# A two-block sequence model on one core: convolution read from the PSUM bank, MLP squares on VectorE, a third x buffer, and all engine queues in another order

## The chip, the cores and the metric

The kernel runs on one core of a Trainium2 chip. The metric is the device time of one execution in microseconds (us). Engines: PE is TensorE (PEld its weight loads), DVE is VectorE, ACT is ScalarE, POOL is GpSimd, SP is SyncE, whose queue issues all DMAs here.

## What is computed

There are 16 sequences ("items") of 256 tokens by 128 features, all in float32. Each goes through the same layers:

```
x1 = x + layernorm(block(layernorm(x)))
out = x1 + layernorm(ffn(layernorm(x1)))
block:
  xm = mix(x);  n = rms_norm(xm);  value, gate = split(n @ in_proj)
  value = silu(causal_conv4(value) + conv_b)
  y = scan(value, A, xm @ B_proj, xm @ C_proj) + D * value
  xm = xm + (y * silu(gate)) @ out_proj
  xm = xm + square(relu(rms_norm(xm) @ m_fc)) @ m_proj
  xa = attention(rms_norm(mix(xm)))          # 16 heads, 4 key/value heads, rope
  xa = xa + square(relu(rms_norm(xa) @ a_fc)) @ a_proj
ffn:  h = silu(x @ w1) * (x @ w2);  h = gelu(h @ h1);  h = gelu(h @ h2);  h @ w3
```

The convolution runs along the tokens with 4 taps per channel: the output at token t uses tokens t-3 to t.

## The kernel before

An item's work is cut into short steps with names (`tin`, `inv`, `bc`, `conv`, ...), each a function of the item `i` and a part `k`. `ORDERS` is a table written out by hand that lists, for each engine, the names in the order in which that engine issues them; `_instances` numbers them, and `run` calls them one after the other. Nothing else sets the order: an engine that waits in one step holds back all that stand behind it in its list. Several items are under way at a time, in different layers. Steps of different engines meet through one semaphore per name (`S[name]`, `at(name, i, k)`).

The eight PSUM banks are handed out by a second table, `BANKS`. `BANKS_OF` says how many banks a PE step claims and which step, on another engine, gives them back; `claim` makes PE wait for that step. All matmuls are recorded at one line (L1170) and all transposes at another (L1187).

The steps that matter here, with their lines before the change:

- `loadx` (SP, L355) brings an item's x into one of two buffers `X`; `st0`, `ag0` (L892, L900), `r1` (POOL, L427 and L430), `xh` (L905), `xm` (L927) make the layer norm; `ss1` (ACT, L600), `r2` (POOL, L437 and L440) and `nrm` (L932, written over `X`) the RMS norm. `tin` transposes both on PE, `xnhi` (ACT, L609) and `xnlo` (DVE, L937) split the result into a high and a low part. Only then can `inv`, `gat`, `bc` (the products with in_proj, B and C) run.
- `va` (ACT, L617) copies the bank of `inv` into `vpad`, whose first three columns are zero. `conv` (DVE, L949 and L951) is the four taps on `vpad`: for two channel halves of 128x256, one tensor_scalar and three scalar_tensor_tensor each. `val` (ACT, L627) is the silu, `vt` and `xp` transpose it.
- `bcx` (ACT, L644) takes B and C out of PSUM, `cb` multiplies them, `m` (DVE, L961 and L962) multiplies with the decay table `LM`, `v` is the product with the values.
- `up`, `relu` (ACT, L668), `sq` (POOL, L476), `down` are the first MLP, `upb`, `relub` (L766), `sqb` (POOL, L512), `downb` the second. `relu` writes `hid` in SBUF, and gives the bank back.
- `mx` (DVE, L1064) are row maxima of the scores, `ex` (ACT, L726) exponentials, `sel` (POOL, L496) the causal masks, `pv` the product with v.
- `glo`, `hlo` (POOL, L542 and L547) write the low parts `gL` for the products `h1` and `h2` (24 matmuls per part each).

Before the first item's bulk work there is preparation: the DVE makes a decay per head in a chain of small operations (`dec`, L828 to L847), ACT and DVE make `LM` from it (`pex` on ACT, L579; `plm` on DVE, L852; 16 operations each), ACT and DVE split the raw weights (`phi`, L584 and L588; `plo`, L862 and L865), DVE folds scales into weights (`fold`), POOL and ACT scale and split the weights of the second network (`fsc`, `flo` on POOL, L414 and L419; `fhi` on ACT, L593).

Of the kernel before, what the change touches and what calls it, by code (L numbers as in the profile page):

```python
# [1510 lines left out]
```

## Time and profile before

| | |
|---|---|
| median of 3 runs | 976.28 us (975.53 to 977.0) |
| the profiled execution | 976.42 us |
| its span in the trace | 974.7 us |
| mean granted TensorE clock | 0.988 of full speed |
| busy: PE / DVE / ACT / POOL | 91% / 69% / 59% / 47% of the span |
| DMA | 8 tenths busy in the first fortieth of the span, 1 tenth in the second, 0 after |

The page of the profile gives each engine's busy time and forty slices of the span. The stretches say the same for windows that one chooses. The waits say for whom an engine stood idle. The timeline lists instructions by start time, with the idle time before them and who ended it in square brackets; merged rows have a count (x16). A group's row gives busy time and mean duration in ns.

### The profile page before, as it was taken

The page shows a single profiled execution, that of the slowest core. Times are in us where ns is not written, and L with a number is a line of the kernel's source. Part 1 is how long each engine was busy: PE and PEld are TensorE (multiplying, and loading weights), DVE is VectorE, ACT ScalarE, POOL GpSimd, SP SyncE. Part 2 cuts the span into 40 slices and gives each one's busy share as a digit, 9 for nine tenths or more (in the row PEclk, how much of TensorE's full clock was granted, in tenths as well). Part 3 has the DMA queues.
Part 4 walks back from the last instruction along what each step waited for, and adds up shares of the span by engine and source line. Part 5 has one row for each costly group of instructions (what it writes and reads, how often), then busy time and mean ns, then how long its engine had stood idle before and what let it go on. Part 6 is the DMA issues. An engine that isn't in the chain of part 4 may idle for free.

```text
span 974.7 us, 24913 instructions
## 1 busy us (share of the span) xinstructions
PE 888.5 (91%) x9248; PEld 758.0 (78%) x9248; DVE 667.8 (69%) x1803; ACT 578.2 (59%) x1220; POOL 460.0 (47%) x708
## 2 busy tenths in 40 slices
PE   0689989999999999998999999999999999989785
PEld 0667768787979888987878898888877887878575
DVE  5978969866777767758576884875776686746320
ACT  3644365766747557746565768567475575575532
POOL 1574344625543637435345545355263644463432
PEclk9999999999999999999999999999999999999899
DMA  8100000000000000000000000000000000000000
GB/s 280 59 17 7 7 7 2 7 1 13 7 13 7 13 2 7 13 12 6 12 7 2 17 2 12 8 12 7 12 2 2 2 13 1 13 1 13 12 3 9
DMA packets 17926, 15.71 MB, mean 16 GB/s; under 512 B 2064, under 2 KB 15760, under 8 KB 17552
## 3 DMA queue, kind: packets, MB, share of 16 engines
q1 hardware_dynamic: 17808, 14.12, 4.6%
q8 instruction: 76, 1.25, 0.5%
q14 instruction: 42, 0.34, 0.1%
HBM read 12.02 MB, written 2.10 MB: 14 GB/s over the span
## 4 chain that ended last, share of the span: by engine, by line
PE 64%; DVE 22%; issue 7%; ACT 3%; POOL 2%; DMA 1%; SPq 0%; POOLq 0%; DVEq 0%; ACTq 0%
PE pool L1170 59%; PE pool L1187 5%; DVE mneg L1064 2%; DVE val L951 2%; DVE M L961 1%; DVE M L962 1%; ACT PT L726 1%; DVE W L1018 1%; DVE val L949 1%; DVE gAB L1144 1%; DVE W L1020 1%; POOL PT L496 1%; DMA X<-in_x 1%; DVE LM L852 1%; DVE val L968 1%
## 5 line engine op out<-in xcount | busy, mean ns | idle before, releaser
L1064 DVE TENSOR_REDUCE mneg<-pool 128x2 f32<-128x512 f32 (+1 forms) x192 | 119.0, 683 | 54.7 <-PE pool L1170 54.7
L1170 PE MATMUL pool<-gH,w_h_hi 128*128 128x256 f32 x512 | 149.1, 291 | 4.8 <-POOL gL L542 2.2
L1170 PE MATMUL pool<-gL,w_h_hi 128*128 128x256 f32 x512 | 143.8, 281 | 0.0
L1170 PE MATMUL pool<-gH,w_h_lo 128*128 128x256 f32 x512 | 143.8, 281 | 0.0
L961 DVE TENSOR_TENSOR M<-pool,LM 128x512 f32<-128x512 f32 x128 | 87.6, 685 | 55.2 <-PE pool L1170 54.8
L726 ACT ACTIVATE PT<-pool 128x512 f32<-128x512 f32 x192 | 99.2, 603 | 31.8 <-PE pool L1170 31.5
L1170 PE MATMUL pool<-BC 64*128 64x256 f32 (+1 forms) x1024 | 111.4, 345 | 3.3 <-ACT PT L726 1.7
L496 POOL TENSOR_SCALAR_AFFINE_SELECT PT<-PT 128x256 f32<-128x256 f32 (+1 forms) x192 | 89.2, 488 | 42.4 <-ACT PT L726 39.0
L1170 PEld LDWEIGHTS pool<-BC 64*128 64x128 f32 x1024 | 87.6, 187 | 26.1 <-issue 14.1
L644 ACT ACTIVATE BC<-pool 128x512 f32<-128x512 f32 x128 | 75.6, 603 | 54.2 <-PE pool L1170 50.9
L1170 PEld LDWEIGHTS pool<-gH,w_h_hi 128*128 128x128 f32 x512 | 96.9, 189 | 7.2 <-issue 3.2
L1170 PEld LDWEIGHTS pool<-gL,w_h_hi 128*128 128x128 f32 x512 | 97.0, 189 | 0.2
L1170 PEld LDWEIGHTS pool<-gH,w_h_lo 128*128 128x128 f32 x512 | 96.8, 189 | 0.0
L542 POOL TENSOR_TENSOR gL<-gAB,gH 128x512 fp32r<-128x512 f32 x32 | 41.3, 1301 | 65.2 <-ACT gH L787 64.9
L547 POOL TENSOR_TENSOR gL<-gAB,gH 128x512 fp32r<-128x512 f32 x32 | 41.0, 1286 | 50.1 <-ACT gH L801 50.0
L1170 PE MATMUL pool<-M,xpad 128*32 128x256 f32 (+1 forms) x1024 | 54.8, 332 | 3.6 <-DVE M L962 3.6
L1170 PE MATMUL pool<-PT,Va 128*32 128x128 f32 (+1 forms) x1024 | 53.2, 338 | 5.1 <-POOL PT L496 5.1
L806 ACT ACTIVATE gAB<-pool 128x512 f32<-128x512 f32 x32 | 19.1, 598 | 63.5 <-PE pool L1170 63.4
L951 DVE SCALAR_TENSOR_TENSOR val<-vpad,cols,val 128x256 f32<-128x256 f32 x96 | 54.9, 612 | 0.4
L962 DVE TENSOR_TENSOR M<-pool,LM 128x256 f32<-128x256 f32 x128 | 53.0, 414 | 0.0
L1170 PE MATMUL pool<-xnH,w_B_hi 128*128 128x256 f32 x128 | 44.0, 344 | 4.4 <-DVE M L962 3.9
L512 POOL TENSOR_TENSOR hid<-hid 128x512 f32<-128x512 f32 x32 | 33.5, 1051 | 29.7 <-ACT hid L766 29.7
(235 smaller groups left out, 2428.0 us busy)
## 6 DMA issues: line engine op xcount, KB each, us to landing
X<-in_x SPq DMA_DIRECT2D x16, 128.0 KB, 2.1
x<-in_x SPq DMA_DIRECT2D x16, 128.0 KB, 2.2
out<-ob SPq DMA_DIRECT2D x16, 128.0 KB, 2.1
hid<-in_w_h SPq DMA_DIRECT2D x1, 1024.0 KB, 8.9
gAB<-in_w_h SPq DMA_DIRECT2D x1, 1024.0 KB, 9.4
PT<-in_w_B SPq DMA_DIRECT2D x1, 512.0 KB, 4.9
PT<-in_w_C SPq DMA_DIRECT2D x1, 512.0 KB, 6.4
Qs<-in_s SPq DMA_DIRECT2D x1, 512.0 KB, 5.0
```

The costliest lines, as they stand in the source:

```text
L496: g.affine_select(w, w, pattern=[[0, w.shape[1]], [1, P]], compare_op=ALU.is_ge, fill=0.0, base=0, channel_multiplier=-1).then_inc(S["sel" ...
L512: g.tensor_tensor(h, h, h, ALU.mult).then_inc(S["sqb"], 1)
L542: g.tensor_tensor(gL[:, J], gA[:, J], gH[:, J].bitcast(F32), ALU.subtract).then_inc(S["glo"], 1)
L547: g.tensor_tensor(gL[:, J], gB[:, J], gH[:, J].bitcast(F32), ALU.subtract).then_inc(S["hlo"], 1)
L644: a.activation(BC[:, n % NBC, :], bank("bc", i, k), ACT.Copy).then_inc(S["bcx"], 1)
L726: a.activation(PT[:, n % NPT, :], bank("e", i, k // 4, k % 4), ACT.Exp).then_inc(S["ex"], 1)
L951: last = v.scalar_tensor_tensor(dst, vpad[:, b, k:k + L], w, dst, ALU.mult, ALU.add)
L961: v.tensor_tensor(M[:, n % NM, :, 0:L], pool8[:, b:b + 2, 0:L], LM[:, 2 * k:2 * k + 2, :], ALU.mult)
L962: v.tensor_tensor(M[:, n % NM, :, L:3 * P], pool8[:, b:b + 2, L:3 * P], LM[:, 2 * k:2 * k + 2, 0:P], ALU.mult).then_inc(S["m"], 1)
L1064: v.reduce_max(dst, o, axis=AX.X, negate=True).then_inc(S["mx"], 1)
L1170: return p.matmul(o, lhsT, rhs, start=start, stop=True, skip_group_check=True)
L1187: last = p.transpose(o[:, k * P:(k + 1) * P], src(k), ident[:])
```

## The change

1. `va` and `vpad` are gone. `conv` reads the bank of `inv` itself. Tap 0 is now the one without a shift and writes all 256 columns with the bias; taps 1 to 3 read columns 0 to 255-k and add to columns k onwards, so no padding is needed. The bank is given back by the last `conv` instead of `va`.
2. `sq` and `sqb` go from POOL to DVE: one scalar_tensor_tensor of 128x512 computes max(bank, 0) times `hid`. ACT's relu stays. The banks of `up` and `upb` are now given back by `sq` and `sqb`.
3. `X` has three buffers; x of items 0 to 2 is loaded at the start. `rows` is loaded third instead of fifth, w_in no longer waits for it, and `m01` (DVE) waits for the first group of transfers only.
4. `xr` (POOL) has one more wait, for its own earlier step.
5. All five lists of `ORDERS` and the bank table are other ones.

```diff
-    tin=(1, "xnlo"), inv=(1, "va"), ...
-    t2=(1, "t2c"), up=(1, "relu"), ... upb=(1, "relub"),
+    tin=(1, "xnlo"), inv=(1, "conv"), ...
+    t2=(1, "t2c"), up=(1, "sq"), ... upb=(1, "sqb"),
...
         def conv(i, k):
-            if k == 0:
-                dve.wait_ge(S["va"], at("va", i))
+            if k == 0:
+                dve.wait_ge(S["inv"], at("inv", i))
...
             for b in range(2):
-                w, dst = cols[:, C_CW + b * KC + k:C_CW + b * KC + k + 1], val[:, i % 2, b, :]
+                c = C_CW + b * KC + KC - 1 - k
+                src, dst = halves(bank("inv", i))[:, b, 0:L - k], val[:, i % 2, b, k:]
                 if k == 0:
-                    last = v.tensor_scalar(dst, vpad[:, b, 0:L], w, cols[:, C_CB + b:C_CB + b + 1], ALU.mult, ALU.add)
+                    last = v.tensor_scalar(dst, src, cols[:, c:c + 1], cols[:, C_CB + b:C_CB + b + 1], ALU.mult, ALU.add)
                 else:
-                    last = v.scalar_tensor_tensor(dst, vpad[:, b, k:k + L], w, dst, ALU.mult, ALU.add)
+                    last = v.scalar_tensor_tensor(dst, src, cols[:, c:c + 1], dst, ALU.mult, ALU.add)
...
-        def va(i, _):
-            act.wait_ge(S["inv"], at("inv", i))
...
-            a.activation(vpad[:, :, KC - 1:], halves(bank("inv", i)), ACT.Copy).then_inc(S["va"], 1)
...
-        def sq(i, k):
-            pool.wait_ge(S["relu"], at("relu", i, k))
-            h = hid[:, 0, 2 * k:2 * k + 2, :]
-            g.tensor_tensor(h, h, h, ALU.mult).then_inc(S["sq"], 1)
+        def sq(i, k):
+            dve.wait_ge(S["relu"], at("relu", i, k))
+            h = hid[:, 0, 2 * k:2 * k + 2, :]
+            v.scalar_tensor_tensor(h, halves(bank("up", i, k)), 0.0, h, ALU.max, ALU.mult).then_inc(S["sq"], 1)
...
-            if i >= 2:
-                sp.wait_ge(S["tin"], at("tin", i - 2))
-            sp.dma_start(X[:, i % 2], xt_v[:, i * T:(i + 1) * T, :]).then_inc(S_x[i % 2], 16)
+            if i >= 3:
+                sp.wait_ge(S["tin"], at("tin", i - 3))
+            sp.dma_start(X[:, i % 3], xt_v[:, i * T:(i + 1) * T, :]).then_inc(S_x[i % 3], 16)
...
         sp.dma_start(heads[:], t["heads"]).then_inc(in_h, 16)
+        sp.dma_start(rows[:], t["rows"]).then_inc(in_h, 16)
...
-        for dst, src in ((rows[:], "rows"), (cols[:], "cols"), (raw_in, "w_in"), (ident[:], "c_ident")):
+        for dst, src in ((ident[:], "c_ident"), (raw_in, "w_in"), (cols[:], "cols")):
...
+        loadx(2, 0)
```

Of the table for PE, the last-but-one line of names before and now (the last items' h1, upb, h2, downb, e, pv):

```
before: "w1 w1 t4 qt qt kt o t5 s upb h1 h1 s upb s h2 mt h2 e downb w3 pv e pv e t6 w1 w1 pv w2 w2 yt t4 o h1 t5 h1 upb upb "
now:    "yt w1 w2 t4 w2 kt qt qt o s s h1 s t5 h1 mt upb e upb h2 downb e pv h2 e w3 t6 pv w1 w1 w2 pv w2 yt t4 o h1 t5 h1 "
```

**ACT at the start.** `LM<-xr,sc` are the 16 exponentials of the decay table, `xnH` is the high part that item 0's bulk products wait for, `BC` the first copies of B and C. Before:

```order
L584 ACTIVATE w_in_hi<-yv 128x512
L588 ACTIVATE w_B_hi<-PT 128x1024
L600 ACTIVATE junk,ssq<-xm 128x128 x2
L588 ACTIVATE w_C_hi<-PT 128x1024
L579 ACTIVATE LM<-xr,sc 128x256 x16
L609 ACTIVATE xnH<-pool 128x512
L617 ACTIVATE vpad<-pool 128x2x256
```

And now:

```order
L593 ACTIVATE junk,ssq<-xm 128x128 x2
L577 ACTIVATE w_in_hi<-yv 128x512
L581 ACTIVATE w_B_hi<-PT 128x1024
L572 ACTIVATE LM<-xr,sc 128x256 x2
L581 ACTIVATE w_C_hi<-PT 128x1024
L602 ACTIVATE xnH<-pool 128x512
L572 ACTIVATE LM<-xr,sc 128x256 x6
L629 ACTIVATE BC<-pool 128x512
```

The high part now stands behind 2 exponentials instead of 16, and the sum of squares (`junk`) ahead of the weight splits.

**DVE at the start.** From the first weight's low part to the low part of item 0 (`xnL`). Before:

```order
L932 TENSOR_SCALAR X<-xm,rsd 128x128 x2
L865 TENSOR_TENSOR w_C_lo<-PT,w_C_hi 128x1024
L852 SCALAR_TENSOR_TENSOR LM<-LM,sc,xr 128x256 x16
L937 TENSOR_TENSOR xnL<-pool,xnH 128x512
L870 SCALAR_TENSOR_TENSOR t4s<-t4s,rows 128x128
```

And now:

```order
L917 TENSOR_SCALAR X<-xm,rsd 128x128 x2
L847 TENSOR_TENSOR w_in_lo<-yv,w_in_hi 128x512
L850 TENSOR_TENSOR w_B_lo<-PT,w_B_hi 128x1024
L850 TENSOR_TENSOR w_C_lo<-PT,w_C_hi 128x1024
L877 BN_STATS bst<-X 128x6 x2
L922 TENSOR_TENSOR xnL<-pool,xnH 128x512
L837 SCALAR_TENSOR_TENSOR LM<-LM,sc,xr 128x256 x4
```

The 16 operations on `LM` stand behind `xnL`, and so do the statistics of item 1 (`bst`), which before stood ahead of item 0's `xh`.

**POOL near the end.** From the masks of item 15 (`PT`) to its second norm. Before:

```order
L496 AFFINE_SELECT PT<-PT 128x512 x4
L542 TENSOR_TENSOR gL<-gAB,gH 128x512 x2
L504 TENSOR_TENSOR rin<-ssq,eps_rms 128x2
L507 TENSOR_TENSOR rsd<-rin,minus 128x2
L547 TENSOR_TENSOR gL<-gAB,gH 128x512
L512 TENSOR_TENSOR hid<-hid 128x512 x2
L547 TENSOR_TENSOR gL<-gAB,gH 128x512
```

And now:

```order
L535 TENSOR_TENSOR gL<-gAB,gH 128x512 x2
L540 TENSOR_TENSOR gL<-gAB,gH 128x512
L554 TENSOR_TENSOR ob<-ob,x 128x256
L502 TENSOR_TENSOR rin<-ssq,eps_rms 128x2
L505 TENSOR_TENSOR rsd<-rin,minus 128x2
L540 TENSOR_TENSOR gL<-gAB,gH 128x512
```

The two squares (`hid`) are no longer between the halves of `gL`.

## Rows read from the trace of the kernel before

**Rows 1.** The page: busy time of each engine, share of the span, instructions.
```profile
PE 888.5 (91%) x9248; PEld 758.0 (78%) x9248; DVE 667.8 (69%) x1803; ACT 578.2 (59%) x1220; POOL 460.0 (47%) x708
```
**Rows 2.** Stretches: us, busy PE, PEld, DVE, ACT, POOL, PEclk, DMA share, GB/s.
```profile
0.00:30.00 30.00, 1.37 (x5) 1.03 (x6) 18.29 (x65) 11.90 (x27) 5.25 (x17) 1.00 0.83 274
30.00:100.00 70.00, 61.47 (x558) 52.07 (x557) 55.92 (x134) 35.76 (x83) 44.80 (x54) 0.95 0.03 9
100.00:200.00 100.00, 92.32 (x1048) 75.24 (x1045) 84.28 (x218) 58.68 (x138) 44.59 (x74) 1.00 0.02 6
200.00:850.00 650.00, 634.69 (x6755) 542.87 (x6755) 465.21 (x1252) 410.98 (x860) 310.54 (x483) 0.99 0.03 8
850.00:975.00 125.00, 98.62 (x892) 86.74 (x890) 44.10 (x137) 60.90 (x113) 54.80 (x83) 0.96 0.03 7
```
**Rows 3.** Waits of PE over the whole span: us in total, times, longest.
```profile
PE pool L1170 <- DVE M L962: 7.9, 8, 3.9
```
**Rows 4.** Timeline of the first 30 us: start, us, engine, line, operation.
```profile
2.26 0.43 SPq L371 DMA_DIRECT2D xr<-in_c_causal  x1
...
4.67 0.18 DVE L828 TENSOR_SCALAR sc<-heads 128x16 f32<-128x16 f32 x1 [1.10 <-DMA xr<-in_c_causal]
...
11.56 1.06 ACT L588 ACTIVATE w_B_hi<-PT 128x1024 fp32r<-128x1024 f32 x1 [3.87 <-DMA PT<-in_w_C]
...
11.98 0.48 DVE L892 BATCH_NORM_STATS2 bst<-X 128x6 f32<-128x128 f32 x2 [6.57 <-DMA X<-in_x]
...
15.12 0.17 DVE L840 TENSOR_TENSOR sc<-sc 128x16 f32<-128x16 f32 x1
15.32 0.17 DVE L841 TENSOR_SCALAR sc<-sc 128x16 f32<-128x16 f32 x1
...
21.15 6.49 ACT L579 ACTIVATE LM<-xr,sc 128x256 f32<-128x256 f32 x16 [1.67 <-DVE sc L847]
...
22.56 6.41 DVE L852 SCALAR_TENSOR_TENSOR LM<-LM,sc,xr 128x256 f32<-128x256 f32 x16
...
27.55 0.57 ACT L609 ACTIVATE xnH<-pool 128x512 fp32r<-128x512 f32 x1
28.89 0.68 DVE L937 TENSOR_TENSOR xnL<-pool,xnH 128x512 fp32r<-128x512 f32 x1
...
29.72 0.55 PE L1170 MATMUL pool<-xnH,w_in_hi 128*128 128x256 f32 x1 [6.98 <-DVE xnL L937]
```
**Rows 5.** Instructions on tile val: duration in ns min/median/max, first and last start.
```profile
L951 DVE SCALAR_TENSOR_TENSOR val<-vpad,cols,val x96: 457/479/1515, 33.3 to 784.6; 128x256 f32<-128x256 f32 x96
...
L968 DVE SCALAR_TENSOR_TENSOR val<-val,cols,pool x32: 470/476/482, 52.5 to 846.2; 128x256 f32<-128x256 f32 x32
```
**Rows 6.** Groups: busy us, mean ns, idle before and by whom.
```profile
L951 DVE SCALAR_TENSOR_TENSOR val<-vpad,cols,val 128x256 f32<-128x256 f32 x96 | 54.9, 612 | 0.4
L949 DVE TENSOR_SCALAR val<-vpad,cols 128x256 f32<-128x256 f32 x32 | 16.7, 564 | 5.6 <-ACT vpad L617 5.6
L1144 DVE TENSOR_TENSOR gAB<-pool,gAB 128x512 f32<-128x512 f32 x32 | 21.4, 683 | 13.2 <-ACT gAB L781 6.7 <-PE pool L1170 6.5
L1064 DVE TENSOR_REDUCE mneg<-pool 128x2 f32<-128x512 f32 (+1 forms) x192 | 119.0, 683 | 54.7 <-PE pool L1170 54.7
```
**Rows 7.** Timeline of DVE, convolution of item 1.
```profile
54.13 2.10 DVE L949 TENSOR_SCALAR val<-vpad,cols 128x256 f32<-128x256 f32 x2 [0.32 <-ACT vpad L617]
...
56.31 5.55 DVE L951 SCALAR_TENSOR_TENSOR val<-vpad,cols,val 128x256 f32<-128x256 f32 x4
```
**Rows 8.** Timeline of PE and POOL near the end.
```profile
910.76 1.93 PE L1170 MATMUL pool<-PT,Va 128*32 128x256 f32 x16 [2.67 <-POOL PT L496]
...
916.33 0.38 PE L1170 MATMUL pool<-x6H,w_hi 128*128 128x256 f32 x1 [2.29 <-DVE x6L L1138]
...
933.14 2.03 POOL L512 TENSOR_TENSOR hid<-hid 128x512 f32<-128x512 f32 x2
935.23 2.05 PE L1170 MATMUL pool<-w_apj,hid 128*128 128x128 f32 x16 [2.33 <-POOL hid L512]
```

More of the change, by code:

```diff
@@ L32 @@
     yt=1, t4=1, o=1, t5=1, upb=2, downb=1, t6=1, w1=2, w2=2, h1=2, h2=2, w3=1,
-    ss1=1, xnhi=1, va=1, ga=1, val=1, xp=1, bcx=8, ss2=1, t2c=1, relu=2, ss3=1, t3c=1, qk=1, vv=1, qtc=2, ktc=1,
+    ss1=1, xnhi=1, ga=1, val=1, xp=1, bcx=8, ss2=1, t2c=1, relu=2, ss3=1, t3c=1, qk=1, vv=1, qtc=2, ktc=1,
     ex=12, yv=1, t4c=1, ss4=1, t5c=1, relub=2, t6hi=1, sl=2, ghi=2, ge1=2, hhi=2, ge2=2,
@@ L40 @@
 BANKS_OF = dict(
-    tin=(1, "xnlo"), inv=(1, "va"), gat=(1, "ga"), vt=(1, "xp"), bc=(1, "bcx"), cb=(2, "m"), v=(1, "yg"), out=(1, "xm2"),
-    t2=(1, "t2c"), up=(1, "relu"), down=(1, "xa"), t3=(1, "t3c"), qkv=(1, "rp"), qt=(1, "qtc"), kt=(1, "ktc"), s=(4, "mx"),
-    mt=(1, "qm"), e=(4, "ex"), pv=(1, "yv"), yt=(1, "yn"), t4=(1, "t4c"), o=(1, "xa2"), t5=(1, "t5c"), upb=(1, "relub"),
+    tin=(1, "xnlo"), inv=(1, "conv"), gat=(1, "ga"), vt=(1, "xp"), bc=(1, "bcx"), cb=(2, "m"), v=(1, "yg"), out=(1, "xm2"),
+    t2=(1, "t2c"), up=(1, "sq"), down=(1, "xa"), t3=(1, "t3c"), qkv=(1, "rp"), qt=(1, "qtc"), kt=(1, "ktc"), s=(4, "mx"),
+    mt=(1, "qm"), e=(4, "ex"), pv=(1, "yv"), yt=(1, "yn"), t4=(1, "t4c"), o=(1, "xa2"), t5=(1, "t5c"), upb=(1, "sqb"),
     downb=(1, "xa3"), t6=(1, "t6lo"), w1=(1, "sl"), w2=(1, "gt"), h1=(1, "ge1"), h2=(1, "ge2"), w3=(1, "ln3"))
@@ L99 @@
-        "ga xp ge2 ss2 ge2 t2c bcx ss1 bcx bcx bcx bcx ktc qtc qtc ss4 relu relu t5c xnhi relub va relub ga bcx bcx val ss2 "
[7 rows of a table removed]
+        "pxx ss1 phi phi pex phi xnhi pex pex pex bcx pex pex bcx bcx pex pex bcx val ga bcx ss1 xp bcx fhi bcx xnhi bcx fhi "
+        "fhi bcx fhi fhi bcx bcx bcx val bcx bcx xp ss2 bcx t2c fhi bcx relu relu ss1 ga fhi xnhi t3c ss3 qk vv bcx bcx ga "
+        "bcx t2c fhi fhi relu relu ss2 bcx bcx bcx val ss1 xp ss3 t3c qk ktc qtc qtc bcx bcx xnhi bcx bcx bcx ex ex ex ex ga "
[7 rows of a table added]
@@ L107 @@
+        "sl val sl ga relu t4c ghi bcx xp bcx bcx ghi ss1 t5c ss4 bcx ktc bcx qtc qtc ge1 ge1 hhi hhi relub relub ex ex ex ex "
[11 rows of a table added]
+        "ex ex bcx bcx bcx val yv vv t6hi xp bcx bcx sl sl ga qtc ktc qtc bcx bcx ghi ghi t4c bcx ss4 ge1 hhi ge1 t5c hhi ex "
[6 rows of a table added]
     ),
     DVE=(
-        "st0 dec ag0 st0 ag0 xh m01 dec xh dec plo dec xm dec plo dec nrm plo plm plm plm plm plm plm plm plm xnlo fold fold "
[34 rows of a table removed]
+        "st0 dec ag0 m01 dec xh dec xm dec dec dec nrm plo plo plo st0 xnlo plm plm ag0 plm fold conv conv conv xh m plm conv "
[36 rows of a table added]
@@ new lines @@
+        "sel hlo hlo sel sel sel sel r7 r4 r4 r7 sel sel sel sel r8 r8 glo glo hlo hlo r5 r5 outp sel sel sel sel sel r6 r6 "
+        "sel x1 sel sel r7 r7 sel sel sel sel r8 r8 glo glo hlo outp r5 r5 hlo r6 r6 x1 r7 r7 glo glo hlo hlo r8 r8 outp r8 "
+        "r8 outp"
+    ),
+    SP=(
+        "loadx loadx loadx loady loady loadx loadx loadx loadx store loady loady loadx store store loady loadx store loadx "
+        "loady loady store loady loadx store store loadx loady loady loadx store store loady store loady store loady loady "
+        "store store loady loady store store store"
@@ L217, in _banks @@
             per = PER[giver]
-            last = 0 if name == "qkv" else per - 1 if name in HELD or name in ("yt", "mt") or per == 1 else k * count + j if count == 4 else k
+            last = 0 if name == "qkv" else per - 1 if name in HELD or name in ("inv", "yt", "mt") or per == 1 else k * count + j if count == 4 else k
             holder[b] = (giver, i, last)
@@ L385, in _ @@
             sp.dma_start(dst, t[src]).then_inc(in_e, 16)
-        run("SP", dict(loadx=lambda n, _: loadx(n + 2, _), loady=loady, store=store))
+        run("SP", dict(loadx=lambda n, _: loadx(n + 3, _), loady=loady, store=store))
         sp.wait_ge(S_out, 16 * BATCH)
@@ L466, in xr_ @@
             elif k == 1:
+                if i >= 1:
+                    pool.wait_ge(S["xr"], at("xr", i - 1))
                 pool.wait_ge(S["xm2"], at("xm2", i))
@@ L507, in r5 @@
                 g.tensor_tensor(rsd[:, 4, i % 2], rin[:, 4], minus1[:], ALU.pow).then_inc(S["r5"], 1)
-        def sqb_(i, k):
-            pool.wait_ge(S["relub"], at("relub", i, k))
-            h = hid[:, 1, 2 * k:2 * k + 2, :]
-            g.tensor_tensor(h, h, h, ALU.mult).then_inc(S["sqb"], 1)
         def r6(i, k):
@@ L561, in outp @@
             g.tensor_tensor(ob[:], ob[:], x1[:, i % 2], ALU.add).then_inc(S["outp"], 1)
-        run("Pool", dict(zero=zero, fsc=fsc, flo=flo, r1=r1, r2=r2, gp=gp, r3=r3, xr=xr_, sq=sq, r4=r4, sel=sel, r5=r5, sqb=sqb_, r6=r6,
+        run("Pool", dict(zero=zero, fsc=fsc, flo=flo, r1=r1, r2=r2, gp=gp, r3=r3, xr=xr_, r4=r4, sel=sel, r5=r5, r6=r6,
                          x1=x1_, r7=r7, glo=glo, hlo=hlo, r8=r8, outp=outp))
@@ L806, in ge2 @@
             a.activation(gA[:, 2 * k:2 * k + 2, :], halves(bank("h2", i, k)), ACT.Gelu).then_inc(S["ge2"], 1)
[L808 removed]
+        run("Activation", dict(pxx=pxx, pex=pex, phi=phi, fhi=fhi, ss1=ss1, xnhi=xnhi, ga=ga, val=val_, xp=xp, bcx=bcx, ss2=ss2, t2c=t2c,
                                relu=relu, ss3=ss3, t3c=t3c, qk=qk, vv=vv, qtc=qtc, ktc=ktc, ex=ex, yv=yv_, t4c=t4c,
@@ L931, in nrm @@
             for k in range(T):
-                last = v.tensor_scalar(X[:, i % 2, k, :], xm[:, i % 2, k, :], rsd[:, 1, i % 2, k:k + 1], float(np.sqrt(D)), ALU.mult, ALU.mult)
+                last = v.tensor_scalar(X[:, i % 3, k, :], xm[:, i % 2, k, :], rsd[:, 1, i % 2, k:k + 1], float(np.sqrt(D)), ALU.mult, ALU.mult)
             last.then_inc(S["nrm"], 1)
@@ L987, in xa_, with sqb_ @@
             last.then_inc(S["xa"], 1)
+        def sq(i, k):
+            dve.wait_ge(S["relu"], at("relu", i, k))
+            h = hid[:, 0, 2 * k:2 * k + 2, :]
+            v.scalar_tensor_tensor(h, halves(bank("up", i, k)), 0.0, h, ALU.max, ALU.mult).then_inc(S["sq"], 1)
+        def sqb_(i, k):
+            dve.wait_ge(S["relub"], at("relub", i, k))
+            h = hid[:, 1, 2 * k:2 * k + 2, :]
+            v.scalar_tensor_tensor(h, halves(bank("upb", i, k)), 0.0, h, ALU.max, ALU.mult).then_inc(S["sqb"], 1)
         def e2(i, _):
@@ L1198, in tin @@
             if i == 0:
-                pe.wait_ge(in_a, 16 * 4)
+                pe.wait_ge(in_a, 16 * 3)
             pe.wait_ge(S["nrm"], at("nrm", i))
             o, = claim("tin", i)
-            turn(o, lambda k: (xm if k < T else X)[:, i % 2, k % T, :], 2 * T).then_inc(S["tin"], 1)
+            turn(o, lambda k: xm[:, i % 2, k, :] if k < T else X[:, i % 3, k - T, :], 2 * T).then_inc(S["tin"], 1)
         def inv(i, _):
```

82 lines of the change are left out of this document (31 added, 51 removed), and 182 rows, old and new, of tables (Activation, DVE, PE, Pool).

## The prediction

> **What bounds the kernel now.** I read the busy times first: PE has work in flight for 888.5 us, 91% of the span, DVE for 69%, POOL for 47% [rows 1]. No part of the change adds or removes a matmul, so the 888.5 stays and what can move is the rest, 974.7 - 888.5 = 86 us in which PE stands idle. The stretches tell where it lies [rows 2]: 28.6 us in the first 30, 8.5 from 30 to 100, 7.7 from 100 to 200, 15.3 in the 650 us from 200 to 850, and 26.4 in the last 125. So the start and the end hold two thirds of it, and the long middle is 98% full: there a faster DVE or POOL step buys little. In the fill from 30 to 200 the waits name the decay product `M` first, with 7.9 us over the whole run [rows 3], and DVE is busy 140.2 of 170 us, 82% [rows 2].
>
> The timeline of the start shows what the 28.6 us are [rows 4]. DVE stands still for 6.57 us for the x of item 1, though item 0's `xh` is next behind it. Then ACT runs 16 exponentials (6.49 us) ahead of `xnH`, DVE 16 products (6.41 us) ahead of `xnL`, and PE starts its bulk work at 29.72.
>
> **The start, worked out.** DVE begins its chain when `diff` and `causal` are there: 4.67 before, and now one DMA issue (0.43) later, at 5.1 [rows 4]. What it must do until `xnL` is the work of the first 30 us without what moved behind: 18.29 [rows 2], less 0.5 of statistics done before 5.1, 6.41 for the `LM` products, about 0.5 for the first weight fold and 0.8 for item 1's aggregate and `xh`, which makes 10.1. Some 40 small operations start 0.20 apart and take 0.17 [rows 4], 1.3 more in all; with half a microsecond for waits DVE is through at 17.1. Is something else later? ACT: w_B arrives where it did, ACT splits it from 11.56 to 12.6, two exponentials take 0.8, w_C's split again 1.06, `xnH` 0.57: 15.1, so ACT is not last. POOL's two small norm steps lie beside DVE's chain. PE starts 0.15 after `xnL`, at 17.3, and that is **12.4 us earlier** than 29.72.
>
> Of the moved DMAs, `rows` goes ahead by two places and x of item 2 is added ahead of the later weights, so these come one issue, 0.43 us, later. They are used tens of us behind their arrival; if that cover were gone the cost is 0.4. The third `X` buffer is worth nothing by itself: the trace has no wait for x after the one above.
>
> **DVE's and POOL's work.** The convolution with both operands in SBUF takes 479 ns in the median but up to 1515, on average 612; the like operation that has one operand in PSUM (`yg`) never took over 482 [rows 5, 6]. Item 1's convolution shows it: 2.10 and 5.55 us for six operations [rows 7], with POOL busy beside it, where 476 each would be 2.9. So I price all 128 taps at 476: 96 x (612 - 476) = 13.1 and 32 x (564 - 476) = 2.8, DVE saves 15.9. VectorE: DVE Perf Modes of the Trainium skill, section on the TRN2 errata, speaks against this: its table gives an operand in PSUM 120 fixed cycles against 58 in SBUF at 0.96 GHz, an estimated 65 ns more per instruction. Rows 5 do not show it: 476 and 479 are the same. By the rule an item's eight taps would cost 0.5 us more, which over the six items of the fill makes the sum 3 us longer, 962; by the row nothing is added.
>
> The squares: a 128x512 product with a bank is 683 ns [rows 6]; two halves of 476 would be 952 [rows 5]. I take 720, nearest to the row of the same size. 64 of them are 46 us, DVE goes to 667.8 + 46 - 16 = 698 and POOL loses a comparable amount. ACT loses the 16 copies `va`; PE never waits for them, so that is worth nothing.
>
> **The fill, 30 to 200.** If PE starts 12.4 us earlier, DVE must be that much denser. Counted in the lists, about ten squares (7 us) fall in this part, and six items' convolutions save six sixteenths of 15.9, 6 us: even. DVE had 158.5 us of work by 200, 11 of it now lie before 17.3, so 147.5 stand in 170: 87% instead of 82%. That is close to full for an engine that serves in order. I let the start give back 2 us for it, and take 2 us off for the collisions like those of rows 7, which were in the way of the waits for `M` [rows 3]. Together: 0, bounds +6 (half the gain is lost) and -8 (half the fill's 16.2 idle us go).
>
> **The middle.** Its idle time is 15.3 in 650 us; the new lists may halve it or add as much as DVE's greater load costs. A bank is held longer now: `inv`'s through eight taps (3.8 us) instead of one copy, `up`'s until the square. I take 0, with -4 and +5.
>
> **The end.** Three waits [rows 8]: 2.67 for the masks, 2.29 for `x6L`, 2.33 for the squares. The PE list now has an h2 part (24 products, near 2.9 us) behind the first `pv` there, and both queues have lost the squares. That covers the first two by half or more: 3 us. POOL's two squares took 2.03; DVE's second one is done 0.72 after relu, so `downb` starts about 1 us earlier. And with `t6` ahead of `w3` the last `x6L` is hidden, 1 us. Together **5 us**, bounds 2 and 7.
>
> **Sum.** 976.4 of the profiled execution (span 974.7 and 1.7 around it; the median of the runs is 976.3, the same) - 12.4 + 0 + 0 - 5 = **959**.
>
> **The rivals.**
> A. *DVE eats the start.* With 87% load PE meets a late `M` or `xnL` more often until the attention of the first items is in step; the start keeps 6 us, the end 2: 968. For it: DVE is the most loaded engine beside PE just there, and PE's largest wait is for it. Against: from 100 to 200 it was busy 84% and PE idle only 7.7% [rows 2].
> B. *The squares come late: slower.* A square stands in DVE's list behind what else is there, often row maxima of 683 ns [rows 6]. Each of 32 `down` products then starts later, where before POOL had the square alone. Two maxima ahead are 1.37 us; if PE is exposed to one of them each time, 32 x 0.68 = 22 us, and the middle gives 959 + 22 = 981. It decides from 17.4 / 32 = 0.54 us exposed per product. Against: POOL's square took about 1.0 by itself, and PE waited for a square in only one notable place [rows 8].
> C. *The lists pack better.* Fill and middle lose half of their idle time, 8 and 4 us: 947. Nothing in the rows speaks for it but the size of the idle time.
> D. *No change.* The 12.4 us are only moved: the second network's weights, whose preparation keeps POOL busy 44.8 of 70 us [rows 2], hold everything where it was. Against: the first item's bulk work needs none of them. 976.
>
> **Chances.** Forecast 0.60 (its own range 953 to 965), A 0.17, B 0.09, C 0.11, D 0.03. The range runs from 947, C's value, to 971, a little past A's, where A keeps less; outside remain B, D and the edge of C. A measurement here tells about 0.2% (2 us) from no change. Faster by more: forecast, A, C and nothing else, 0.88; within: 0.03; slower: 0.09.
>
> **What would show it.** PE's first bulk product at 16 to 19 us, with `xnL` just before it. Convolution taps at a mean near 480 with no long ones, squares near 720, DVE near 698 us busy, POOL near 390. PE idle from its start until about 190 us no more than 16 us; the middle as full as before; the last stretch some 5 us shorter. I am wrong if PE's waits for `hid` or for `M` on DVE exceed ten microseconds, if the taps from PSUM are not near 480, or if the start comes and the fill swallows it.

## The result and the profile after

The changed kernel takes **923.4 us** (median of 4 runs, 920.98 to 926.01), the kernel before 975.9 on the same chip: ratio 0.9461, interval 0.9432 to 0.949. That is 52 us less, where the forecast was 17 and its range ended at 947.

The page of the changed kernel, its busy times, to be read beside [rows 1]:

```profile
PE 876.6 (95%) x9248; PEld 754.2 (82%) x9248; DVE 670.8 (73%) x1867; ACT 550.5 (60%) x1192; POOL 383.7 (42%) x643
```

The same matmuls now count 876.6 us as busy instead of 888.5. DVE has 64 operations more and is hardly busier. The stretches of the changed kernel, same cuts and columns as [rows 2] (the last cut lies at 925, since the kernel is over by then):

```profile
0.00:30.00 30.00, 12.68 (x88) 11.34 (x88) 23.27 (x80) 16.91 (x35) 4.33 (x15) 1.00 0.80 279
30.00:100.00 70.00, 62.13 (x646) 51.05 (x642) 59.79 (x160) 32.00 (x83) 37.98 (x52) 0.95 0.04 11
100.00:200.00 100.00, 98.11 (x1075) 81.72 (x1074) 82.19 (x216) 65.56 (x145) 42.96 (x73) 1.00 0.02 4
200.00:850.00 650.00, 644.78 (x6962) 557.22 (x6962) 484.76 (x1349) 400.79 (x868) 268.09 (x459) 1.00 0.03 8
850.00:925.00 75.00, 58.88 (x486) 52.84 (x484) 20.80 (x66) 35.19 (x61) 30.34 (x46) 0.96 0.04 12
```

In the stretch from 200 to 850 PE was 98% busy and is now 99%, which looks like nothing. But in the same 650 us it does 6962 matmuls instead of 6755.

Equal clock times compare different work. So here are both kernels again, cut where PE has issued the same number of matmuls: the first 5 or 6, the next 1605 to 1609, the 6752 to 6756 after them, the last 881 or 882, counted by their starts. The order on PE differs a little between the two, the amount doesn't (a row also counts a matmul that only reaches into its stretch, hence its slightly larger counts). The kernel before, columns as in [rows 2]:

```profile
0.00:30.10 30.10, 1.47 (x6) 1.13 (x7) 18.39 (x65) 11.90 (x27) 5.25 (x17) 1.00 0.83 273
30.10:200.60 170.50, 154.29 (x1610) 127.70 (x1609) 140.09 (x351) 95.04 (x221) 90.00 (x128) 0.98 0.02 7
200.60:850.90 650.30, 634.99 (x6757) 543.29 (x6757) 466.11 (x1254) 410.38 (x860) 310.84 (x483) 0.99 0.03 8
850.90:975.00 124.10, 97.72 (x884) 85.84 (x882) 43.20 (x135) 60.90 (x113) 53.90 (x82) 0.96 0.03 8
```

The changed kernel:

```profile
0.00:17.80 17.80, 1.46 (x6) 1.11 (x7) 11.21 (x45) 8.60 (x19) 3.06 (x13) 1.00 0.80 257
17.80:182.40 164.60, 153.90 (x1608) 127.38 (x1608) 142.28 (x381) 97.06 (x226) 77.28 (x117) 0.98 0.09 30
182.40:811.20 628.80, 625.51 (x6757) 540.13 (x6756) 468.86 (x1299) 382.95 (x842) 257.60 (x442) 1.00 0.03 8
811.20:925.00 113.80, 95.72 (x889) 85.54 (x882) 48.46 (x144) 61.84 (x109) 45.75 (x72) 0.97 0.03 8
```

I call these four parts start, fill, middle and end, and use them for every kernel below. Against the spans of 974.7 and 924.2 us they give:

| part | before | after | difference | forecast |
|---|---|---|---|---|
| start | 30.1 | 17.8 | -12.3 | -12.4 |
| fill | 170.5 | 164.6 | -5.9 | 0 |
| middle | 650.3 | 628.8 | **-21.5** | 0 |
| end | 123.8 | 113.0 | -10.8 | -5 |
| span | 974.7 | 924.2 | -50.5 | -17.4 |

What PE waits for in the changed kernel, beside [rows 3]:

```profile
PE pool L1184 <- DVE X L917: 13.6, 1, 13.6
PE pool L1167 <- DVE xnL L922: 4.7, 2, 2.8
PE pool L1167 <- DVE M L949: 2.9, 5, 1.2
PE pool L1167 <- POOL gL L535: 2.2, 1, 2.2
PE pool L1167 <- POOL gL L540: 2.2, 1, 2.2
```

The 7.9 us for `M` are down to 2.9. The start, to be read beside [rows 4]:

```profile
16.61 0.67 DVE L922 TENSOR_TENSOR xnL<-pool,xnH 128x512 fp32r<-128x512 f32 x1
17.20 1.27 DVE L837 SCALAR_TENSOR_TENSOR LM<-LM,sc,xr 128x256 f32<-128x256 f32 x3
17.43 0.55 PE L1167 MATMUL pool<-xnH,w_in_hi 128*128 128x256 f32 x1 [2.77 <-DVE xnL L922]
```

The convolution and the squares (min/median/max in ns), beside [rows 5]:

```profile
L938 DVE SCALAR_TENSOR_TENSOR val<-pool,cols,val x96: 450/474/484, 22.0 to 737.5; 128x255 f32<-128x255 f32 x32, 128x254 f32<-128x254 f32 x32, 128x253 f32<-128x253 f32 x32
L936 DVE TENSOR_SCALAR val<-pool,cols x32: 528/537/546, 21.0 to 734.7; 128x256 f32<-128x256 f32 x32
L979 DVE SCALAR_TENSOR_TENSOR hid<-pool,hid x32: 659/684/694, 63.9 to 799.1; 128x512 f32<-128x512 f32 x32
```

No tap is over 546 ns any more. Taps 1 to 3 are what was forecast (476), the squares a little less (720), tap 0 is more than the 476 put down for it.

### The profile page after: what moved, and what is told of

Read it like the earlier page. It is cut to its first block and busy times, and to the rows that moved or that the text cites. A ratio compares the mean times of both kernels' runs of the same rounds, so it can differ in the third digit from the quotient of the medians.

```text
span 924.2 us, 24882 instructions
## 1 busy us (share of the span) xinstructions
PE 876.6 (95%) x9248; PEld 754.2 (82%) x9248; DVE 670.8 (73%) x1867; ACT 550.5 (60%) x1192; POOL 383.7 (42%) x643
## 5 line engine op out<-in xcount | busy, mean ns | idle before, releaser
L711 ACT ACTIVATE PT<-pool 128x512 f32<-128x512 f32 x192 | 102.3, 603 | 28.7 <-PE pool L1167 28.4
L1167 PE MATMUL pool<-BC 64*128 64x256 f32 (+1 forms) x1024 | 108.0, 345 | 1.9 <-DVE M L949 1.2
L535 POOL TENSOR_TENSOR gL<-gAB,gH 128x512 fp32r<-128x512 f32 x32 | 40.5, 1277 | 72.4 <-ACT gH L772 72.4
L446 POOL TENSOR_TENSOR val<-val,gate 128x512 f32<-128x512 f32 x16 | 20.6, 1285 | 63.2 <-DVE val L955 63.2
L1167 PEld LDWEIGHTS pool<-M,xpad 128*32 128x32 f32 x1024 | 27.7, 110 | 23.0 <-issue 7.0
```

The lines of the kernel that those rows point to most:

```text
L446: g.tensor_tensor(val[:, i % 2], val[:, i % 2], gate[:], ALU.mult).then_inc(S["gp"], 1)
L535: g.tensor_tensor(gL[:, J], gA[:, J], gH[:, J].bitcast(F32), ALU.subtract).then_inc(S["glo"], 1)
L711: a.activation(PT[:, n % NPT, :], bank("e", i, k // 4, k % 4), ACT.Exp).then_inc(S["ex"], 1)
L1167: return p.matmul(o, lhsT, rhs, start=start, stop=True, skip_group_check=True)
```

## The experiments

The theories at the outset: *lists* (the new order alone brings the gain, by start, end and better packing) against *edits* (the convolution and the squares bring it, either because a latency on PE's way goes, or because DVE operations no longer collide with POOL's). Unless said otherwise a variant starts from one kernel, has its lists, and puts a step that comes back where its input was ready in the trace. The variants ran on three chips, on which the kernel before took 979.3 to 979.8 us. The changed kernel, run again on one of them, gave 0.9442 (0.941 to 0.9474), 923.0 us, and differences of variants are taken to that ratio, times 979 us; with intervals of 0.3% on each side they are good to some 4 us.

### after_again: the changed kernel on this chip

> The changed kernel itself once more, on the chip and in the rounds of the two kernels that follow, since the variants so far ran on another chip than it did. If chips differ no more than the kernel before does (975.9 on one, 979.5 on the other), the ratio to it stays within 0.943 to 0.949, 921 to 929 us.

Measured: 922.98 us, ratio 0.9442. Its span is 3.7 us shorter than that of the first profile, and the fill is where it lies:

```profile
17.60:178.80 161.20, 150.98 (x1608) 126.04 (x1608) 141.19 (x381) 97.28 (x226) 77.50 (x117) 1.00 0.09 30
```

The granted clock was 0.998 over this execution and 0.993 over the first, 1.00 against 0.98 in the fill. What the clock fell short of is (1 - 0.993) x 924.2 = 6.5 us in the first and 1.8 in this one, 4.7 apart, near the 3.7. So a few us between two executions are clock alone. For the kernel before the same sum is 0.012 x 974.7 = 11.7, so of the 50.5 us it can explain 5.2, a tenth.

### new_neither: the new lists without the two edits

```diff
+        def va(i, _):  ...  a.activation(vpad[:, :, KC - 1:], halves(bank("inv", i)), ACT.Copy)
-                src = halves(bank("inv", i))[:, b, 0:L - k]
+                src = vpad[:, b, k:k + L]
-            v.scalar_tensor_tensor(h, halves(bank("up", i, k)), 0.0, h, ALU.max, ALU.mult)
+            g.tensor_tensor(h, h, h, ALU.mult)
```

> The changed kernel's lists, x buffers and DMA order, with both edits of the arithmetic undone: the convolution reads a padded copy that ACT makes again, the squares are on POOL again, each put into its list where the trace of the changed kernel has its input ready. Lists theory (the order and the bank table bring nearly all of the 52 us): 923 to 932 us. Edits theory (taps that no longer collide with POOL and squares off POOL are what lets PE run full): 945 to 965 us, with PE idle for M and hid again. Long taps (over 1 us) come back in both.

Measured: 954.27 us, ratio 0.9759 (0.9723 to 0.9796). The lists, third buffer and DMA order bring 24 us, the two edits on top of them 31. Cut at the same matmuls:

```profile
0.00:17.40 17.40, 1.40 (x5) 1.05 (x6) 11.15 (x45) 8.54 (x19) 3.54 (x14) 1.00 0.85 264
17.40:193.60 176.20, 157.62 (x1607) 129.51 (x1607) 149.55 (x371) 100.41 (x232) 90.08 (x127) 0.97 0.08 28
193.60:837.30 643.70, 628.14 (x6757) 539.87 (x6755) 460.17 (x1251) 388.72 (x852) 312.24 (x490) 1.00 0.03 8
837.30:950.00 112.70, 93.64 (x893) 83.92 (x882) 44.62 (x138) 61.79 (x109) 51.69 (x78) 0.99 0.03 8
```

So the lists give the start (-12.7) and the end (-11.5: 112.3 of the span of 949.6), lose 5.7 in the fill, and 6.6 come off the middle. The edits then give 11.6 in the fill and 14.9 in the middle, and nothing at either end. "Lists" as the whole cause falls. The rows also tell the two shares of the middle apart by kind. With the new lists PE's idle time there stays what it was (650.3 - 635.0 = 15.3 us, now 643.7 - 628.1 = 15.6) and its busy time falls by 6.9; the edits then take 12.3 of the idle time away (628.8 - 625.5 = 3.3 is left) and 2.6 of the busy time. Of the 15.6 us, PE waited 3.8 for POOL's masks and 1.9 for POOL's squares.

### new_vpad: only the convolution from the padded copy again

```diff
-                src = halves(bank("inv", i))[:, b, 0:L - k]
+                src = vpad[:, b, k:k + L]      # and va on ACT
```

> Only the convolution from the padded copy again, all else as changed. Lists theory: 923 to 928. Edits theory: DVE gets its 16 us of collisions back and PE stands for it, 935 to 950.

Measured: 944.29 us, ratio 0.9661 (0.9629 to 0.9692): 21 us slower than the changed kernel. Fill and middle, and the taps:

```profile
17.30:192.50 175.20, 157.32 (x1608) 129.82 (x1608) 151.77 (x381) 100.58 (x232) 80.04 (x117) 0.97 0.08 29
192.50:829.10 636.60, 626.62 (x6758) 539.70 (x6755) 475.52 (x1299) 388.35 (x851) 263.63 (x442) 1.00 0.03 8
```

```profile
L947 DVE SCALAR_TENSOR_TENSOR val<-vpad,cols,val x96: 453/485/1509, 21.3 to 754.9; 128x256 f32<-128x256 f32 x96
L945 DVE TENSOR_SCALAR val<-vpad,cols x32: 398/411/1365, 20.5 to 752.0; 128x256 f32<-128x256 f32 x32
```

The fill alone is 10.6 us longer. The long taps are back.

### new_vawait: the copy is made and waited for, and not read

```diff
+        def va(i, _):  ...  a.activation(vpad[:, :, KC - 1:], halves(bank("inv", i)), ACT.Copy)
             if k == 0:
-                dve.wait_ge(S["inv"], at("inv", i))
+                dve.wait_ge(S["va"], at("va", i))
```

> The changed kernel, in which ACT again copies the bank of inv into vpad and tap 0 waits for that copy, but all taps go on reading the bank: nobody reads vpad. DVE's work stays as in the changed kernel (taps near 475 ns, none long); only the way from inv to tap 0 gets longer by ACT's copy and its place in ACT's list. The padded copy with taps that read it gave 944.3, the changed kernel 923.4, so 20.9 us are to be explained. Theory collisions (the 1.5 us taps beside POOL and what they push back on DVE are the 20.9): 923 to 930. Theory latency (the wait for ACT and the copy, some 1 us for each of 16 items, and what is queued behind it on DVE): 938 to 944. Between the two if both hold.

Measured: 932.44 us, ratio 0.9515 (0.9499 to 0.9531). Both hold: waiting for ACT costs 7 us of the 21, reading SBUF instead of the bank the other 14 (net of the bank being given back earlier by the copy).

```profile
18.00:182.90 164.90, 152.92 (x1607) 126.65 (x1607) 141.47 (x381) 99.86 (x232) 77.38 (x117) 0.99 0.09 30
182.90:816.40 633.50, 625.36 (x6757) 539.25 (x6755) 469.43 (x1299) 388.04 (x852) 257.59 (x442) 1.00 0.03 8
```

They lie in different parts. The fill is as short as in the first profile of the changed kernel (164.9 for 164.6), so the 10 us that the padded copy costs there are the collisions and what they bring with them: DVE was busy 151.8 us in it, and is 141.5 without them. An estimated (0.99 - 0.97) x 170 = 3.4 us of the 10 came by way of the granted clock, which was 0.97 there with the padded copy and 0.99 here. The middle is 4.7 us longer than the changed kernel's 628.8: that is the latency. Over the whole run DVE is busy 686.9 us with the padded copy and 670.6 here.

### new_sqpool: only the squares on POOL again

```diff
-            v.scalar_tensor_tensor(h, halves(bank("up", i, k)), 0.0, h, ALU.max, ALU.mult)   # DVE
+            g.tensor_tensor(h, h, h, ALU.mult)                                               # POOL
```

> Only the squares on POOL again. Lists theory: 923 to 928. Edits theory: masks, low parts and squares queue on POOL, 930 to 945. A third way: DVE was the tighter engine, and without the 46 us of squares on it the kernel gets faster, 915 to 921.

Measured: 937.04 us, ratio 0.9577 (0.9538 to 0.9615), 13 us slower than the changed kernel, most of it in the middle:

```profile
184.60:820.10 635.50, 626.80 (x6758) 540.30 (x6756) 452.07 (x1251) 383.26 (x843) 305.70 (x490) 1.00 0.03 8
```

### new_dumsq: squares on DVE, and POOL's work for them kept

```diff
+        def dq(i, k):
+            pool.wait_ge(S["relu"], at("relu", i, k))
+            g.tensor_tensor(dum[:], dum[:], dum[:], ALU.mult)     # 128x512, read by nobody
```

> The changed kernel with DVE's squares, to which POOL gets 64 idle products of 128x512 on a tile of its own at the places where its squares stood in the variant with squares on POOL (937.0 beside 923.4 of the changed kernel, 13.6 us). Each waits for the relu as the square did, and nobody waits for its result. POOL's work then is that of the variant, and PE's way through the square is that of the changed kernel. Theory POOL's load (its queue is late for masks and norms, and it stretches DVE's operations with two SBUF inputs): 933 to 939. Theory path (the product on POOL took 1.0 us on the way from up to down, DVE takes 0.69 and no more): 923 to 927, with POOL near 450 us busy.

Measured: 933.5 us, ratio 0.9532 (0.9508 to 0.9556). Of the 13 us that POOL's squares cost, 9 come from POOL being occupied at these places, though nobody waits for what it makes; 4 are left for the square's own way. PE waits 6.3 us for POOL's masks, which were 1.1 in the changed kernel, and DVE is busy 681.7 us instead of 670, without an operation more:

```profile
PE pool L1182 <- POOL PT L509: 6.3, 8, 1.5
```

### new_actsq: squares on ACT

```diff
-            v.scalar_tensor_tensor(h, halves(bank("up", i, k)), 0.0, h, ALU.max, ALU.mult)   # DVE
+            a.activation(h, h, ACT.Square)                                                  # ACT, right behind relu
```

> The changed kernel with the 64 squares on ACT, right behind each relu, in place of DVE: DVE loses 64 times 0.69 = 44 us, ACT gains about 64 times 0.55 = 35 and goes to 586, POOL stays near 384. No semaphore of another engine lies between relu and square. If DVE's load is what PE waits for in the hidden part of the middle: 910 to 919, faster than the changed kernel. If it is only important that POOL is free: 921 to 926. If ACT's list, made for less, delays the exponentials and copies behind the squares: 927 to 940.

Measured: 941.9 us, ratio 0.9615 (0.9601 to 0.963): 17 us slower than the changed kernel, just over the dearest of the three guesses.

```profile
185.30:827.60 642.30, 629.26 (x6758) 541.90 (x6756) 440.54 (x1251) 412.01 (x891) 258.01 (x442) 1.00 0.03 8
```

In the middle DVE has 28 us less to do than in the changed kernel and ACT 29 more, and the middle is 13.5 us longer. ACT is the least suspicious engine by its share, 64% there, and still 0.63 us more at each square, ahead of its exponentials and copies, shows in PE's time. DVE's load, at 75% of the changed kernel's middle, is not what the middle waits for most. (The run changes both loads at once, so what DVE's relief alone is worth it doesn't tell.)

### old_sq and old_sqsb: the squares on DVE in the old lists

First as in the change, reading the bank; then as a product of `hid` with itself, so that relu gives the bank back as before.

```diff
-            g.tensor_tensor(h, h, h, ALU.mult)                                               # POOL
+            v.scalar_tensor_tensor(h, halves(bank("up", i, k)), 0.0, h, ALU.max, ALU.mult)   # DVE, old_sq
+            v.tensor_tensor(h, h, h, ALU.mult)                                               # DVE, old_sqsb
```

> The kernel before, its lists kept, with the squares on DVE where their input is ready by its trace. Lists theory: within 4 us of 976. Edits theory: 960 to 970. The rival of the prediction that squares come late on DVE: 980 or more.

> The kernel before with the squares on DVE at the same places as in the variant that cost 14 us (ratio 1.014), but as a product of hid with itself, both operands in SBUF, so that the banks of up and upb are given back by relu as before. Theory banks (the 14 us come from banks held until a square behind other DVE work, PE waited 10.6 us for hid there while it had the squares themselves in time): 975 to 983. Theory DVE's load (44 us more in a list that wasn't made for it delay M, the maxima and the norms behind each square): 990 to 1000, at or above the other variant, since with both operands in SBUF the products meet POOL's operations and get longer.

Measured: 991.58 us, ratio 1.0143 (1.0103 to 1.0182), and 988.51 us, ratio 1.0095 (1.0066 to 1.0125). The same edit that gains about 10 in the new lists (new_neither against new_vpad) costs 14 in the old ones (10 to 18 by its interval). In `old_sq`:

```profile
PE pool L1170 <- DVE hid L987: 6.2, 9, 1.8
PE pool L1170 <- DVE hid L982: 4.4, 5, 2.3
```

```profile
202.00:861.90 659.90, 635.57 (x6758) 542.11 (x6758) 483.10 (x1301) 410.42 (x860) 262.61 (x435) 1.00 0.03 8
```

In `old_sqsb` the waits for `hid` are no longer among the seven largest, though its squares meet POOL and get long:

```profile
L982 DVE TENSOR_TENSOR hid<-hid x32: 674/684/1274, 73.6 to 868.7; 128x512 f32<-128x512 f32 x32
L987 DVE TENSOR_TENSOR hid<-hid x32: 676/686/1552, 159.4 to 944.1; 128x512 f32<-128x512 f32 x32
```

Neither theory alone: about 5 of the 14 us go with the banks that are held until the square (the two intervals just overlap, so the 5 is not certain), about 9 are left, which I put down to DVE's load; no run takes that load away alone. And the squares are hardly ever late for their product. I took for each of the 32 `down` and `downb` the time from the end of the last square to the first matmul: the median is 1.9 us in the kernel before and 2.8 in `old_sq`, and PE's idle time right ahead of the 32 is 2.1 us in all. What gets late in `old_sq` is the product that is to have the square's bank next: 8.8 of the 10.6 us of waits above stand ahead of other products than `down` and `downb`. That what stands behind the squares in DVE's list gets late too is argued, not shown.

### new_oldstart and old_newstart: only the start exchanged

The first stretch of the ACT, DVE and POOL lists of one kernel is put on the other; for the second also the DMA order. Of ACT's list:

```diff
-pxx ss1 phi phi pex phi xnhi pex pex pex bcx ...
+pxx phi phi ss1 phi pex pex pex pex pex pex pex pex xnhi bcx ...
```

> The changed kernel with the start of three lists as before (16 exponentials ahead of the high part on ACT, 16 LM products ahead of the low part on DVE, item 1's statistics ahead of item 0's xh); DMA order as changed. PE should start 11 us later, near 28 us. If the start is worth what PE's start moved: 934 us. If the fill catches up with it: 925 to 929.

> The kernel before with the new start alone (lists' heads, DMA order, the earlier wait of m01). The prediction's first term: PE starts near 18 us, the time falls by 12 to 964. If DVE eats the start (rival A): 968 to 972.

Measured: the changed kernel with the old start 932.77 us, ratio 0.952 (0.9494 to 0.9546), 8 us slower; the kernel before with the new start 975.3 us, ratio 0.9966 (0.9944 to 0.9987), 3 us faster. PE's bulk work starts at 29.5 in the one and 17.5 in the other. Start and fill of `new_oldstart`, then the fill of `old_newstart`:

```profile
0.00:29.80 29.80, 1.44 (x6) 1.10 (x7) 18.36 (x65) 11.90 (x27) 4.05 (x15) 1.00 0.84 281
29.80:187.70 157.90, 150.68 (x1608) 125.92 (x1608) 133.56 (x361) 94.05 (x217) 76.02 (x115) 1.00 0.03 8
```

```profile
17.80:197.90 180.10, 159.22 (x1610) 131.35 (x1609) 145.43 (x371) 102.03 (x233) 92.02 (x131) 0.94 0.08 27
```

The 12 us at the start are real in both, and the fill takes a part of them back in both. In the changed kernel it is 6.7 us by its first profile (164.6 against 157.9, at a clock of 0.98 against 1.00) and 3.3 by its second (161.2, at 1.00). In the old lists it is 9.6, but the granted clock of the fill fell from 0.98 to 0.94 there, which makes an estimated 0.04 x 175 = 7 of the 9.6. DVE is no busier in that fill (145 of 180 us, 81%, for 82% before) and PE waits less for `M` in it (6.1 us for 7.7); its waits for ACT's `BC` grew from 1.0 to 4.0.

### new_end: the last item's low parts on DVE

```diff
-            g.tensor_tensor(gL[:, J], gA[:, J], gH[:, J].bitcast(F32), ALU.subtract)   # POOL
+            v.tensor_tensor(gL[:, J], gA[:, J], gH[:, J].bitcast(F32), ALU.subtract)   # DVE, item 15 alone
```

> The changed kernel with one thing moved: the four low parts gL of the last item (two for h1, two for h2) are made by DVE instead of POOL. In the changed kernel each takes POOL 1.28 us, PE waits 2.2 us for them twice, and DVE has next to nothing to do there. A product of 128x512 with one operand in PSUM takes DVE 0.69; with both in SBUF and POOL quiet I expect about the same. The second part of a pair then ends about 1.1 us earlier, set by ACT's copy before it: 2 us over both pairs, so 0.2% below the changed kernel on this chip, 921 to 923 where that gives 924. If the last item's chain has another member close behind: no difference, 923 to 925.

Measured: 920.79 us, ratio 0.9398 (0.9371 to 0.9425), the changed kernel in the same rounds 922.98. The operation takes half as long on DVE, and the last part is 110.0 us (919.9 - 809.9) instead of 113.0:

```profile
L539 POOL TENSOR_TENSOR gL<-gAB,gH x30: 1267/1277/1303, 185.1 to 883.0; 128x512 fp32r<-128x512 f32 x30
L993 DVE TENSOR_TENSOR gL<-gAB,gH x2: 691/692/693, 904.7 to 905.9; 128x512 fp32r<-128x512 f32 x2
```

The 2 us by the medians are what was worked out, but the intervals overlap. What the trace shows surely is that PE's two waits for `gL` fall from 2.2 us each to 1.6 and 1.5. The rest of the 3.0 can be clock: it was 0.99 in this last part, and 0.97 and 0.98 in the two profiles of the changed kernel, 1 to 2 us.

## Why the prediction was wrong

**The start** (-12.4) was right: first bulk product at 17.43 for 17.3, `xnL` just before it, the part 12.3 us shorter.

**The middle** (0, bounds -4 and +5) is the step that failed. It read the 650 us as "98% full: there a faster DVE or POOL step buys little", and so let 4 of the 15.3 us of idle time go at most ("may halve it" would have been 7.7). The middle lost 21.5 us. 12.0 of them are this idle time, which went from 15.3 to 3.3. It was small beside the 650 us, but nearly all of it could be had.

The other 9.5 us are busy time (634.99 - 625.51, with the same matmuls), which the prediction took as fixed ("the 888.5 stays"). Up to 3 of them are clock: the kernel before had a granted clock of 0.97 in two stretches of 50 us there, from 450 and from 800, which the changed one hadn't. The first follows a wait: PE stood 2.44 us until 457.11 for ACT's `val`, and then issued its matmuls 0.21 us apart until 459.95, where 0.12 is usual. For the rest a matmul's row hides short waits. Within one product of the kernel before:

```profile
462.04 0.28 PE L1170 MATMUL pool<-gH,w_h_hi 128*128 128x256 f32 x1
462.16 0.28 PE L1170 MATMUL pool<-gL,w_h_hi 128*128 128x256 f32 x1
```

Such a matmul counts as busy for 0.28 us and the next one starts 0.12 us after it, so PE can stand still for up to some 0.16 us behind it and the row shows none of it. That these hidden waits are the 6 or 7 us left is argued; no run shows them one by one.

PEld, which the page also prints, hides less (a weight load is 0.19 us long): 543.3 of 650.3 us, 84%, before, and 540.1 of 628.8, 86%, now. It is nearly the same number of us in every variant (539 to 542, from the rows of their middles), so it says better than PE's row that there was room. How much, it doesn't say: 650 - 543 = 107 us is no bound that can be reached, since in a run of 16 products with `BC` without a gap PEld shows 1.24 of 1.45 us, 86% (changed kernel, 22.95 to 24.40). The Trainium skill states, in Perfetto Trace Analysis, section Identifying the Most-Contended Engine, that the matmul busy share is no good measure of how near TensorE is to its limit, and that the share of weight loads is to be used beside the useful work. This trace agrees so far as PE's row goes. The reason given there, that pipelined matmuls look smaller in a trace, is not what the rows above show: they look longer, 0.28 for 0.12. The chain of waits gave a second hint. The page of the kernel before has in its part on the chain that ended last

```profile
PE 64%; DVE 22%; issue 7%; ACT 3%; POOL 2%; DMA 1%; SPq 0%; POOLq 0%; DVEq 0%; ACTq 0%
```

so DVE stood on the path for 22% of the span, 214 us, with PE idle in 9%.

Of these 21.5 us, by the runs, 6.6 belong to the lists and 14.9 to the edits. The up to 3 us of clock lie in the lists' part (the clock of the middle was 0.99 before and 1.00 in `new_neither`). Convolution and squares each shorten it alone, too (from 643.7 to 635.5 and to 636.6).

**The fill** (0, bounds +6 and -8) came out at -5.9, within its bounds, and partly by luck: both of its halves were too small, and they have opposite signs. That the fill gives back part of the start is seen in both exchanges (3.3 to 6.7 us in the new lists, 9.6 in the old ones, most of that clock; 2 were taken). That shorter taps help is worth 10 us there, shown by `new_vpad` against `new_vawait` (175.2 against 164.9), with up to 3.4 of the 10 by way of the clock. 2 were taken off, since only the squares' load was weighed against the 6 us of DVE time saved.

**DVE's and POOL's work.** Taps 1 to 3 and squares as forecast (474 and 684 ns for 476 and 720), POOL 383.7 for 390. DVE was to be 698 us busy and was 670.8. 64 x (0.720 - 0.684) = 2 of the 27 are the squares. The larger part is in DVE's other operations, which the prediction took as fixed: added up by duration from the traces, all but taps and squares take 701 us before, 688 in `new_neither` and 675 in the changed kernel. So the new lists bring one half of it, the edits the other. Two of these operations before (groups as in [rows 6]):

```profile
L1018 DVE SCALAR_TENSOR_TENSOR W<-W 128x40 f32<-128x40 f32 x48 | 16.1, 334 | 1.0
L932 DVE TENSOR_SCALAR X<-xm,rsd 128x128 f32<-128x128 f32 x32 | 13.9, 476 | 5.5 <-POOL rsd L440 5.5
```

in `new_neither`, where the new lists still have the squares on POOL:

```profile
L1023 DVE SCALAR_TENSOR_TENSOR W<-W 128x40 f32<-128x40 f32 x48 | 10.9, 227 | 1.1
L936 DVE TENSOR_SCALAR X<-xm,rsd 128x128 f32<-128x128 f32 x32 | 11.8, 408 | 3.1 <-POOL rsd L442 3.1
```

and in the changed kernel:

```profile
L1015 DVE SCALAR_TENSOR_TENSOR W<-W 128x40 f32<-128x40 f32 x48 | 11.0, 229 | 1.1
L917 DVE TENSOR_SCALAR X<-xm,rsd 128x128 f32<-128x128 f32 x32 | 9.0, 324 | 0.0
```

`W` gets short by the new order alone. `X` does so by half, and the rest goes with POOL's 67 us of squares. That POOL's work is the cause of the edits' half is shown from the other side by `new_dumsq`: with 64 products back on a tile of POOL's own, DVE is busy 11 us more.

**The end** (-5, bounds 2 and 7) was -10.8. The lists alone give -11.5, so it is the order, not the squares. I priced three waits there and no more; PE's idle time in this part went from 123.8 - 97.7 = 26.1 us to 113.0 - 95.7 = 17.3.

**The rivals.** C (the lists pack better) was nearest in size, and wrong in the cause: without the edits the new lists save 6.6 us in the middle, none of it idle time, and the fill becomes longer by 5.7. Its sum is off, too: half of the middle's 15.3 us is 7.7 and not 4, which makes it 943. A (DVE eats the start) fits the old lists in size, where 12 us at the start leave 3, and not in its mechanism: what ate them there is the clock more than DVE. B (squares late: slower) is what the squares do in the old lists, +14, but not by its mechanism: PE hardly waits for the squares, it waits for the banks that they hold. ACT's copies `va` were put down as "worth nothing", since PE never waits for them; the wait alone costs 7 us. It passed through DVE, which a list of PE's waits can't show; the group of tap 0 did, with 5.6 us of DVE's idle time put down to `vpad` [rows 6]. The third `X` buffer "worth nothing by itself" wasn't tried: for most items the new DVE list takes the statistics of item i+2 ahead of `nrm` of item i. With two buffers the x of item i+2 could be loaded only after `tin` of item i, which needs that `nrm`. So the third buffer is what allows this order, and its worth, which no run shows by itself, is in the lists.

**What stays open.** The convolution from the bank in the old lists wasn't tried. There the bank of `inv` would be held to the last tap, and whether the old bank table bears that is open. That the edits and lists together are worth more than apart is thus shown for the squares alone. What within the new lists saves the 11.5 us at the end and the 6.6 in the middle wasn't taken apart.

## What to carry to other kernels

A TensorE that is 98% busy in the trace is not full. Ask first whether the 2% can all go (here 12.0 of 15.3 us did), and don't take them for the whole room: short waits and a lower clock lie within the busy time (9.5 us here). Read PEld's share, the matmuls per stretch, or the time between equal counts of matmuls, before writing down that a faster helper buys little; and look who stands in the chain of waits. Compare the granted clock of two stretches before you explain their difference. When an edit takes an operation off an engine on which others wait, or away from operations that it stretches, count all operations that met it, and try the edit and the order apart: here the same edit was worth -10 us in one order and +14 in another.
